# Attention layers of a fused transformer kernel: score matmuls between the feed-forward halves, query features in another bank, layer-norm deviations on ScalarE

## What is computed

```python
def favor(x, omega):                       # features of queries and keys
    xs = x * dh ** (-0.25)
    u = einsum('bshd,dm->bshm', xs, omega)
    h = 0.5 * sum(xs * xs, axis=-1, keepdims=True)
    return concatenate([exp(u - h), exp(-u - h)], axis=-1) * m ** (-0.5)

for l in range(3):
    Qf, Kf, v = favor(out @ Wq[l] + bq[l]), favor(out @ Wk[l] + bk[l]), out @ Wv[l] + bv[l]
    a = causal_linear_attention(Qf, Kf, v)          # sum_{j<=i} (q_i.k_j) v_j / sum_{j<=i} q_i.k_j
    h = layer_norm(out + a @ Wo[l] + bo[l])         # (x - mean) * rsqrt(var + 1e-5) * g + b
    y = relu(h @ W1[l] + bf1[l]) @ W2[l] + bf2[l]
    out = layer_norm(h + y)
```

## Time and profile before

| | us |
|---|---|
| median of three runs | 2030.52 |
| the profiled execution | 2030.56 |
| its span in the profile | 2028.7 |
| attention part, first product input (L1398) to the last slot's start | 628.66 to 1813.42 |
| TensorE busy | 1673.9 (83%) |
| VectorE busy | 1552.6 (77%) |
| ScalarE busy | 882.8 (44%) |
| GpSimd busy | 981.9 (48%) |

### The profile page before, as it was taken

The page is one execution under the profiler, slowest core; times in us unless marked ns, Lnnn a source line. Parts: engine busy times, 40 slices in busy tenths (PEclk is TensorE's granted clock), DMA queues, the critical chain, the costliest instruction groups (busy, mean ns, idle before and its releaser), DMA issues. The chain is left out here.

```text
span 2028.7 us, 67977 instructions
## 1 busy us (share of the span) xinstructions
PE 1673.9 (83%) x28443; PEld 1255.2 (62%) x28445; DVE 1552.6 (77%) x3835; ACT 882.8 (44%) x1642; POOL 981.9 (48%) x1045
## 2 busy tenths in 40 slices
PE   5655555459946999999999999999999999996798
PEld 4333334359944666666666666666666666663798
DVE  2899964459975878878788788778878888885675
ACT  2555555446622444444444444444444444442321
POOL 0677747769953324324334334234324334333797
PEclk9877765579977999999999999999999999997899
DMA  7400001122230000000000000000000000000001
GB/s 207 84 0 0 0 23 33 36 61 64 63 119 1 3 3 3 3 3 3 3 3 3 3 3 3 3 3 3 3 3 3 3 3 3 3 3 1 16 31 37
DMA packets 60715, 42.75 MB, mean 21 GB/s; under 512 B 19720, under 2 KB 54800, under 8 KB 59952
## 3 DMA queue, kind: packets, MB, share of 16 engines
q1 hardware_dynamic: 47504, 25.35, 4.8%
q0 software_dynamic: 4352, 8.99, 1.3%
q10 hardware_dynamic: 8608, 4.67, 0.9%
HBM read 24.22 MB, written 14.77 MB: 19 GB/s over the span
## 5 line engine op out<-in xcount | busy, mean ns | idle before, releaser
L368 POOL TENSOR_TENSOR at_rstd<-at_mv,const 128x4 f32<-128x4 f32 x96 | 19.4, 202 | 555.9 <-DVE at_mv L362 555.9
L1612 PE MATMUL psum<-attn_w,at_qa 128*128 128x128 f32 x1536 | 184.1, 278 | 0.0
L1604 PE MATMUL psum<-at_vT,attn_w 128*128 128x512 f32 x384 | 179.8, 611 | 1.7 <-ACT at_vT L1417 0.9
L1612 PEld LDWEIGHTS psum<-attn_w,at_qa 128*128 128x128 f32 x1536 | 175.2, 192 | 2.6 <-issue 0.5
L1421 ACT ACTIVATE at_qa<-psum,attn_bf 128x512 f32<-128x512 f32 x192 | 131.9, 687 | 89.3 <-PE psum L1604 89.3
L1316 DVE TENSOR_SCALAR at_kb<-at_kf,const 128x512 f32<-128x512 f32 x192 | 157.8, 881 | 0.0
L1322 DVE STREAM_TRANSPOSE at_vb<-at_vT 32x512 uint32<-32x512 uint32 x192 | 134.7, 701 | 1.9
L1838 PE MATMUL psum<-tilesT,ti_masked 128*128 128x128 f32 x1024 | 120.0, 279 | 13.0 <-POOL ti_masked L1800 13.0
L1838 PEld LDWEIGHTS psum<-tilesT,ti_masked 128*128 128x128 f32 x1024 | 117.9, 195 | 14.6 <-issue 14.6
L1546 PE MATMUL psum<-at_state,at_qa 64*64 64x36 f32 x3072 | 115.7, 242 | 8.1 <-issue 7.1
L1425 ACT ACTIVATE at_qa<-at_qf,const 128x512 f32<-128x512 f32 x192 | 122.2, 710 | 0.0
(11 more groups left out here) (303 smaller groups left out, 4306.8 us busy)
## 6 DMA issues: line engine op xcount, KB each, us to landing
ex_xs<-sorted_x SPq DMA_DIRECT2D x80, 65.0 KB
x<-in_L_attn_x ACTq DMA_DIRECT2D x8, 512.0 KB, 7.7
ex_feats<-token_y SPq DMA_DIRECT2D x4, 1024.0 KB, 8.0
out<-x SPq DMA_DIRECT2D x16, 256.0 KB, 2.3
expert_w<-in_L_ffn_w SPq DMA_DIRECT2D x1, 2048.0 KB, 9.0
attn_w<-in_L_attn_W SPq DMA_DIRECT2D x2, 768.0 KB
token_y<-ex_y,ex_place POOLq DMA_INDIRECT x72
sorted_x<-ex_spare SPq DMA_DIRECT2D x1, 1040.0 KB, 7.2
```

What stands on the lines that cost most here:

```text
L1604: mm(bank(f.s, c), k.w1[:, f.l, c * P:(c + 1) * P], hT[f.s][:], start=True, stop=True).then_inc(hid_ready, 1)
L1612: last = mm(bank(f.s, 1)[:, c * D:(c + 1) * D], hidden[f.s][:, t, c * P:(c + 1) * P], k.w2[:, f.l, t, :], start=(t == 0 and c == 0), stop= ...
```

## The change

Seven edits, all but the first in the attention part.

1. ScalarE loads an activation table set that holds logarithm and exponential, at the very start of the kernel, ahead of its first DMA issues.
2. The inverse deviations of the attention part move from GpSimd to ScalarE, as exp(-0.5 * ln(var + eps)): two activations of 128x4.
3. The query features of a are built in bank(1 - s, 3), the other stream's; chunk sums no longer wait for their exponential, the fourth product of L1604 (the one that writes that bank) does.
4. ScalarE takes the input of the feed-forward (L1417) ahead of the exponential of the query features, and makes two of the four masked copies of the query features before the relus.
5. TensorE computes the first half of the scores between the two halves of the second feed-forward product.
6. VectorE masks the first half of the scores before it adds up f's feed-forward result, and the second half before it normalises; the statistics of fresh input come after the running sum.
7. The transposes of the next input wait for one chunk each, not for all four.

```diff
+                nc.scalar.preload_act_table_set("natural_log_exp_and_others")
                 act.dma_start(k.const[:], ins["constants"]).then_inc(mix_loaded, 16)
...
+def inverse_deviation_by_log(nc, st, k, rstd, mv):
+    st.done(nc.scalar.activation(rstd[:], mv[:, :, 1], ACT.Ln, bias=cst(k, "eps")[:, 0:1]))
+    return nc.scalar.activation(rstd[:], rstd[:], ACT.Exp, scale=-0.5)
...
     for c in range(GC):
         last = nc.vector.tensor_scalar(xn[:, c, :], x_of(c), mv[:, c, 0:1], rstd[:, c:c + 1], ALU.subtract, ALU.mult)
+        if chunk_ready:
+            last.then_inc(chunk_ready, 1)
...
# ScalarE's slot
+                    if f:
+                        res_deviation(f, 0)
...
-                        nc.scalar.activation(qf[s][:], bank(s, 3), ACT.Exp, bias=feature_bias[:, 0, l:l + 1]).then_inc(qf_ready, 1)
+                        nc.scalar.activation(qf[s][:], bank(1 - s, 3), ACT.Exp, bias=feature_bias[:, 0, l:l + 1]).then_inc(qf_ready, 1)
+                    if a:
+                        act.wait_ge(qf_ready, n + 1)
+                        masked_queries(s, 0)
...
+                        masked_queries(s, 1).then_inc(qa_ready, 1)
+                        if then and f and f.l == L - 1:
+                            mod_deviation(then)
                         act.wait_ge(state_ready, n + 1)
                         nc.scalar.activation(carry[l][s][:], state[s][:, :, NSUB], ACT.Copy)
+                    if f:
+                        res_deviation(f, 1)
+
+                for s in two:
+                    mod_deviation(FIRST[s])
                 act.wait_ge(wu_ready, 1)
...
# TensorE
-                    pe.wait_ge(*h.input)
                     for c in range(GC):
+                        pe.wait_ge(*h.input[c])
                         last = nc.tensor.transpose(bank(s, 0)[:, c * P:(c + 1) * P], xn[s][:, c, :], ident)
...
-                        mm(bank(s, 3), wu[0][:, l, :], xT[s][:], start=True, stop=False)
+                        mm(bank(1 - s, 3), wu[0][:, l, :], xT[s][:], start=True, stop=False)
...
-                        pe.wait_ge(qf_ready, n + 1)
                         sums(s, 0)
                         sums(s, 1)
                     if f:
                         pe.wait_ge(hT_taken, f.count + 1)
                         for c in range(GC):
+                            if a and c == 3:
+                                pe.wait_ge(qf_ready, n + 1)
...
+                        feed_forward_out(f, 0)
                     if a:
...
                         scores(s, n, 0)
+                    if f:
+                        feed_forward_out(f, 1)
+                    if a:
                         scores(s, n, 1)
...
# VectorE
+                        if then and f and f.l == L - 1:
+                            mod_statistics(then)
+                    if a:
+                        causal(0)
                     if f:
                         s, n = f.s, f.count
...
-                        causal(0)
+                        causal(1)
```

More of the change, by code:

```diff
@@ L1240, in __init__ @@
                 group = turn * HALVES + half
-                self.input = (mod_ready, group * 2 + s + 1) if l == 0 else (xn_ready, (group * (L - 1) + l - 1) * 2 + s + 1)
+                ready, turns = (mod_ready, group * 2 + s) if l == 0 else (xn_ready, (group * (L - 1) + l - 1) * 2 + s)
+                self.input = [(ready, turns * GC + c + 1) for c in range(GC)]
                 self.before = not isinstance(turn, int) or turn + half + l > 0
@@ L1350, in slot @@
                         causal(0)
+                    if f:
+                        s, n = f.s, f.count
+                        dve.wait_ge(hres_ready, n + 1)
+                        dve.wait_ge(ff_ready, n + 1)
+                        st.done(nc.vector.tensor_tensor(flat(res[s][:]), bank(s, 1), flat(hres[s][:]), ALU.add))
+                        statistics(nc, lambda c: res[s][:, c, :], stats[s], mv[s]).then_inc(res_stats, 1)
+                    if a:
+                        causal(1)
                     ends = f and f.l == L - 1
@@ L1391, in _, with mod_deviation, res_deviation, masked_queries @@
             def _(act):
+                st = Steps(act, act_steps, 0)
+                def mod_deviation(h):
+                    act.wait_ge(mod_stats, h.turn + 1)
+                    inverse_deviation_by_log(nc, st, k, xrstd[h.s], xmv[h.s]).then_inc(mod_rstd, 1)
+                def res_deviation(f, i):
+                    act.wait_ge(res_stats, f.count * 2 + i + 1)
+                    inverse_deviation_by_log(nc, st, k, rstd[f.s], mv[f.s]).then_inc(res_rstd, 1)
+                def masked_queries(s, half):
+                    for i in (2 * half, 2 * half + 1):
+                        last = nc.scalar.activation(qa[s][:, :, i, :], qf[s][:].rearrange("p (j i) -> p j i", i=SUB), ACT.Copy,
+                                                    scale=cst(k, "mask_a")[:, i:i + 1])
+                    return last
                 def slot(a, f, then):
@@ L1562, in output_weights, with feed_forward_out @@
                         last.then_inc(wo_ready, 1)
+                def feed_forward_out(f, half):
+                    for t in (2 * half, 2 * half + 1):
+                        pe.wait_ge(hid_taken, f.count * FT + (t + 1 if t != 0 else 2))
+                        for c in range(GC):
+                            last = mm(bank(f.s, 1)[:, c * D:(c + 1) * D], hidden[f.s][:, t, c * P:(c + 1) * P], k.w2[:, f.l, t, :],
+                                      start=(t == 0 and c == 0), stop=(t == FT - 1), skip_group_check=True)
+                    if half:
+                        last.then_inc(ff_ready, 1)
                 def slot(a, f, then):
@@ L1587, in slot @@
                         pe.wait_ge(kq_taken, n * 2 + 2)
-                        mm(bank(s, 3), cst(k, "half"), sqq[s][:], start=False, stop=True).then_inc(feat_ready, 1)
+                        mm(bank(1 - s, 3), cst(k, "half"), sqq[s][:], start=False, stop=True).then_inc(feat_ready, 1)
                     if f:
@@ L1608, in slot @@
                     if f:
-                        for t in range(FT):
-                            pe.wait_ge(hid_taken, f.count * FT + (t + 1 if t != 0 else 2))
-                            for c in range(GC):
-                                last = mm(bank(f.s, 1)[:, c * D:(c + 1) * D], hidden[f.s][:, t, c * P:(c + 1) * P], k.w2[:, f.l, t, :],
-                                          start=(t == 0 and c == 0), stop=(t == FT - 1), skip_group_check=True)
-                        last.then_inc(ff_ready, 1)
+                        feed_forward_out(f, 0)
                     if a:
```

47 lines of the change are left out of this document (12 added, 35 removed).

## The result

| | before | changed |
|---|---|---|
| median, us | 2028.61 (4 runs) | 2004.93 (2003.68 to 2005.25, 4 runs) |
| profiled execution, its span | 2030.56, 2028.7 | 2005.25, 2003.4 |
| 46 slots after the first, mean | 25.24 | 24.57 |
| commonest slot without a stall | 24.34 | 24.34 |
| idle "issue" of TensorE in these 46 slots | 30.0 | 4.1 |

The ratio is 0.9882, 95% interval 0.9865 to 0.990. The forecast was 2011 us, the time 2004.93. The total was well met and its composition was not: the 46 slots got 30.9 us shorter, of which 25.9 us are fetch stalls (idle time marked "issue") and about 5.1 us time at a reduced clock (an estimate: three stretches, 10.2 us in all, at a granted clock of 0.50, that is 1.2 GHz, with half of it lost). All the rest of the slots together gave nothing.

A forecast was written before the change was run, and what follows sets the result against it. TensorE was taken to bound the attention slots until their last 2 us, where VectorE's chain is as late. Terms 8.3 + 7.2 + 2.4 + 1.8 + 3.0 - 1.0 - 1.7 = 20.0 us off 2030.56 gave 2011 us, range 1992 to 2030.

The forecast's parts named there:

- Query features in the other bank: Ordinary attention slots: first feed-forward matrix starts 0.26 us earlier as chunk sums stop waiting; 32 slots, 8.3 us gained.
- Scores between the halves and the slot's end: Attention slots: two more tile-shape changes at 0.1 us each; next slot starts f+10.3 to 10.4, level with 10.42; nothing counted.
- rival C: Attention slots: tile-shape changes cost 0.85 us a slot, not 0.2; 30 us slower, 2041 us; chance 0.08.
- Deviations on ScalarE: Around layer stacks' ends: 7.2 us in 8 slots, 2.4 in the 8 before; last slot 1.8; ordinary slots no time.
- Fetch stalls: TensorE's "issue" idle: 7.1 us at L1546 nearly goes, 3 us counted; 20.4 us at L1553 stays.
- Start and table set: Kernel start: table load ahead of DMA issues loses 1.0 us; attention part's start: late weight copy loses 1.7 us.
- The forecast's own signs: In the attention part: no chunk-sum wait, matrix 0.26 us earlier, slots 23.8 at best, 24.8 on average, L1546's stalls gone.
- rival B: Attention part: stalls nearly all go, and clock dips with them; another 25 to 30 us, 1984 us; chance 0.1.
- D: Attention slots: the query-feature wait reappears elsewhere at full size, start's losses stand; 2028 us; chance 0.07.
- A: Attention slots: fetch stalls take back half of the 17.9 us of slot gains; 2022 us; chance 0.2.

The follow-up runs named there:

- e3: Kernel before with edits 3 and 4 alone (query features in the other bank, ScalarE's order with it): 2018.02 us, ratio 0.9964.
- e1: Changed kernel with edits 5 and 6 undone (scores in one piece behind the second feed-forward matrix, VectorE's old order): 2008.65 us, ratio 0.9911.
- e9: Changed kernel with the third group of chunk sums put between third and fourth product of the first feed-forward matrix: 2005.03 us, ratio 0.9894.
- e4: Changed kernel with the attention part's deviations back on GpSimd: 2021.36 us, ratio 0.9973.
- e2: Kernel before with edits 5 and 6 alone (divided scores and VectorE's order that goes with them): 2069.5 us, ratio 1.0205.
- e10: Changed kernel with mended start and undivided order in 23 attention slots, those in which that order had stalls: 2012.81 us, ratio 0.9939.
- e6: Changed kernel with GpSimd's preparation waiting for the first inputs' statistics, ScalarE's weight copy still behind the deviations: 1997.81 us (1 run).
- e5: Changed kernel with GpSimd's preparation waiting for the first inputs' statistics and ScalarE's weight copy ahead of the deviations: 1997.36 us, ratio 0.9868.

## Why the total was met, and which steps of the prediction failed

- **Query features in the other bank, +8.3 us.** The step is right by itself: 0.26 us at the first matrix, and e3's slot is 0.25 shorter. In the whole change it bought nothing, since the slot's end took it back.
- **Scores between the halves and the slot's end, "level", nothing counted.** This failed. e1 shows a cost of 0.52 us a clean slot against the undivided order, between the 0.2 taken on TensorE and the 0.85 of rival C. On TensorE it is 0.35; and the end of the slot was put at f+10.3 to 10.4 and is at f+10.67. Part of that was a slip in adding up. VectorE's addition came at f+3.94 before (873.80 - 869.86); with 0.96 for the first scores and 0.2 for two changes it is f+5.10, not 4.92, and from there, by the step's own terms, the normalisation ends at f+9.38, not 9.12. Measured are 5.23 and 9.41. So by the forecast's own numbers the next slot starts near f+10.6, and most of the gain of 0.26 was already spent. Told apart by runs: a change of tile shape by itself 0.03 (e9), the division on TensorE 0.35, the wait behind VectorE 0.17.
- **Deviations on ScalarE.** The size of the pair was right: 0.52 us. VectorE's wait came down to 0.74 and not to 0.5. That the step "buys VectorE room and no time" in an ordinary slot was wrong: with both masks ahead of the normalisation VectorE's chain ends the slot, and e4 shows 0.40 us each in the clean slot. Behind a stack's end the forecast gave 9.6 us for 16 slots; 15 of those (all but the first of the part) went from 379.5 to 372.8 us, 6.7 us, of which 5.0 are stalls. In the last slot 1.8 us were forecast. There both waits of VectorE for a deviation fell by 0.81 us, 1.6 in all, as these lines of its second one show, before and after:

```profile
1860.91 1.12 DVE L375 TENSOR_SCALAR at_qf<-at_kt,at_mv,at_rstd 128x128 f32<-128x128 f32 x4 [1.41 <-POOL at_rstd L369]
...
1834.59 1.11 DVE L382 TENSOR_SCALAR at_qf<-at_kt,at_mv,at_rstd 128x128 f32<-128x128 f32 x4 [0.60 <-ACT at_rstd L376]
```

At the kernel's end only 0.3 us of it are left (214.29 us from the last first product before, 214.03 after, a stretch that varies from 212.0 to 216.1 over the twelve profiles).

- **Fetch stalls, 3.0 us.** This failed most: 25.9 us went, and 5.1 of reduced clock with them. The step said that the stalls at L1553 stay because the run of weighted values is unchanged. It looked at the time of the last block alone. A stall there is the debt of the whole run since the first scores, as e1, e2 and e10 show, and the division cuts that run in two. The forecast's own pace, 3.57 us for 256 instructions, would have given this, had it been added up over the run. The Trainium skill (Runtime: NRT & Kernel Launch, Instruction fetch mechanics) calls the cost mostly hidden; the traces disagree wherever small matmuls stand close: 30.0 us before, and the size of a block agrees.
- **Start and table set, -2.7 us.** The copy's place was seen (1.5 us measured, 1.7 forecast). That GpSimd no longer waits for statistics, and so starts its preparation beside VectorE, was missed: 2.2 us (e6). The 1.0 us for the table set was not lost: the load runs from 0.70 to 1.98 us, and ScalarE's first DMA issue still begins at 0.73, where it began at 0.70 with the load behind it.

The sum on record is 20.0 us, the measured one 23.7, and that they are close is luck. In the profiled executions, which are 25.3 us apart, about 31.0 are stalls and clock where 3.0 was forecast, nothing more comes from the slots taken together where 17.9 was, -3.7 comes at the start where -2.7 was, and -2.0 is the spread ahead of the attention part. The terms that were missed happened to cancel.

The forecast's own signs told it. The chunk sums' wait went, the matrix came 0.26 us earlier and L1546's stalls went, as they should. But slots near 23.8 at best and 24.8 on average became 24.34 and 24.57, and "issue" under 10 us was the sign of rival B. B had this outcome, with a chance of 0.1 and no reason for it: beyond the 3.0 us counted, 28 us of stalls and clock went, in its 25 to 30. Its total of 1984 was still missed, for what the slots and the start did not give. D was right for the ordinary slots, whose gain came back as waits at the slot's end, and missed the stalls. A falls, since the stalls did go. C was right in direction, with a price of 0.52 us a slot instead of 0.85, and was outweighed.

## What to carry to other kernels

Add up instructions over the whole run between two long operations and compare with the pace of the fetches; in this kernel a stall stands where the run ends, not where it is caused. Breaking a run with a long operation removed the stall here but had a price in every repetition, so do it only where a trace shows the stall. When a step is moved off an engine, look at what that engine now starts earlier, and beside whom.

## What had not been expected of the hardware

- Fetches of 16 KB of instructions begin 3.25 us apart or more in each of the twelve kernels, also where TensorE idles for the next one, and the stalls of the kernel before end 2.2 to 3.0 us after one began.
- A VectorE step of 0.17 us took 2.34 us beside a GpSimd step of 2.35 us on two SBUF operands, ending with it, and four of 1.12 us together took 4.04; with GpSimd kept back both are at their size again (e5, e6). Not every step is hit: VectorE's statistics of 0.86 us, beside GpSimd's next two steps (623.05 us), kept their size.
- A divided run of matmuls cost more where 128-column products stand beside 64x64 tiles (0.35 us) than where 512-column ones stand beside 32x32 tiles (0.05 us).
